# An LRU layer and a routed feed-forward on one core: the final stage adds both expert results to x1 in PSUM, and statistics and scaling read PSUM

## The reference

```python
x = _layernorm(x + LRU(x))      # x + x + sigmoid(res_logit) * gelu(y @ W1) @ W2, y from a complex linear recurrence
x = _layernorm(x + FFN(x))      # the stage of the change
# FFN: softmax over 8 experts, the two best per token, each with its weight
for e in range(8):
    h = gelu_exact(xf @ W1[e] + b1[e]);  y = h @ W2[e] + b2[e]
    out = out + y * cw[:, e:e + 1]
# _layernorm(x) = (x - mean) / sqrt(var + 1e-5) over the 128 features
```

## Time and profile before

| what | value |
|---|---|
| runs of the kernel before | 400.19, 402.85, 404.06 us; median 402.85 |
| the profiled execution, span from its first to its last instruction | 403.5 us |
| busy: PE, DVE, ACT, POOL | 75%, 73%, 64%, 65% of the span |
| indirect DMAs issued by POOL | 64 of L431, 108 of L437 |
| instructions | 6693 |

### The profile page before, as it was taken

The page is one execution under the profiler, slowest core; times in us unless marked ns, Lnnn a source line. Parts: engine busy times, 40 slices in busy tenths (PEclk is TensorE's granted clock), DMA queues, the critical chain, the costliest instruction groups (busy, mean ns, idle before and its releaser), DMA issues.

```text
span 403.5 us, 6693 instructions
## 1 busy us (share of the span) xinstructions
PE 301.3 (75%) x1531; PEld 253.2 (63%) x1531; DVE 295.8 (73%) x787; ACT 259.8 (64%) x569; POOL 263.2 (65%) x297
## 2 busy tenths in 40 slices
PE   2368999869874788899993599999999999100440
PEld 1235777546653677799993599999999995000110
DVE  3998999998653799899995289999999995100160
ACT  3315688378563687899994389999999993000451
POOL 4793479508877010577787777877877777777560
PEclk9999999899996699899999599999999999855585
DMA  4736516700111210223321332333333361111772
GB/s 116 268 95 220 173 39 220 281 1 33 48 47 37 56 42 20 67 74 88 87 69 54 85 92 79 85 85 83 84 89 89 92 199 52 52 52 52 190 215 78
DMA packets 47627, 39.23 MB, mean 97 GB/s; under 512 B 5160, under 2 KB 40240, under 8 KB 47608
## 3 DMA queue, kind: packets, MB, share of 16 engines
q1 hardware_dynamic: 42104, 27.68, 23.9%
q0 software_dynamic: 5504, 11.35, 8.6%
HBM read 18.39 MB, written 20.62 MB: 97 GB/s over the span
## 4 chain that ended last, share of the span: by engine, by line
POOL 32%; PE 29%; DVE 13%; issue 13%; ACT 6%; DMA 5%; SPq 0%; DVEq 0%; ACTq 0%; POOLq 0%
POOL slots_d L431 17%; POOL results_d L437 13%; PE bank L1016 8%; PE bank L1018 7%; PE bank L1017 7%; PE bank L1102 2%; DVE work L688 1%; PE bank L1119 1%; ACT fw L611 1%; DMA late<-slots_d 1%; DMA slots_d<-rows,slot_i 1%; ACT h L515 1%; DVE wuse L878 1%; DVE work L682 1%; DMA logs<-in_L_attn_res_logit_dram 1%
## 5 line engine op out<-in xcount | busy, mean ns | idle before, releaser
L437 POOL DMA_INDIRECT results_d<-work,dest x108 | 119.2, 1103 | 33.0 <-issue 32.0
L431 POOL DMA_INDIRECT slots_d<-rows,slot_i x64 | 72.1, 1127 | 49.4 <-DVE rows L834 19.1
L569 ACT ACTIVATE h<-bank,buse 128x384 f32<-128x384 f32 x144 | 84.1, 584 | 7.1 <-PE bank L1018 3.7
L915 DVE TENSOR_TENSOR h_l<-h,h_h 128x384 fp32r<-128x384 f32 x144 | 80.0, 556 | 6.3 <-ACT h_h L574 3.3
L1016 PE MATMUL bank<-h_h,wuse 128*128 128x384 f32 (+1 forms) x176 | 70.6, 401 | 3.9 <-DVE h_l L915 2.4
L1017 PE MATMUL bank<-h_l,wuse 128*128 128x384 f32 (+1 forms) x176 | 62.0, 352 | 0.0
L1018 PE MATMUL bank<-h_h,wuse 128*128 128x384 f32 (+1 forms) x176 | 61.9, 352 | 0.0
L1016 PE MATMUL bank<-xt_h,wuse 128*128 128x384 f32 x144 | 50.6, 351 | 3.7 <-ACT h L569 2.4
L878 DVE CAST wuse<-fw 128x1024 fp32r x72 | 49.8, 692 | 0.8 <-issue 0.8
L1017 PE MATMUL bank<-xt_l,wuse 128*128 128x384 f32 x144 | 49.5, 344 | 0.0
L1018 PE MATMUL bank<-xt_h,wuse 128*128 128x384 f32 x144 | 49.5, 344 | 0.0
(11 more groups left out here) (204 smaller groups left out, 651.8 us busy)
## 6 DMA issues: line engine op xcount, KB each, us to landing
late<-slots_d SPq DMA_DIRECT2D x36, 195.0 KB
late<-in_L_ffn_W_dram SPq DMA_DIRECT2D x16, 256.0 KB, 2.8
slots_d<-zeros SPq DMA_DIRECT2D x3, 1300.0 KB, 7.8
slots_d<-zeros SPq DMA_DIRECT2D x3, 1040.0 KB, 6.8
work<-results_d SPq DMA_DIRECT2D x10, 256.0 KB, 5.5
work<-in_L_attn_x3d_dram SPq DMA_DIRECT2D x8, 256.0 KB, 3.4
out_dram<-fw SPq DMA_DIRECT2D x8, 256.0 KB, 3.1
results_d<-work,dest POOLq DMA_INDIRECT x108
```

The lines of the kernel that those rows point to most:

```text
L431: pool.indirect_dma_start(out=slots_d, out_offset=bass.IndirectOffsetOnAxis(ap=slot_i[:, k, i:i + 1], axis=0), in_=rows[:, k, i, :], in_of ...
L437: pool.indirect_dma_start(out=results_d, out_offset=bass.IndirectOffsetOnAxis(ap=dest[:, SQ * g + q:SQ * g + q + 1], axis=0), in_=yo[:, g ...
L569: act.activation(h32[:, b % 2, 0:SLOTS], H_PS[b % 2][:, 0:SLOTS], ACT.Gelu, bias=buse[:, k, b:b + 1]).then_inc(sm["gelu_b"], 1)
L915: dve.tensor_tensor(ht_l[b], h32[:, b % 2, 0:SLOTS], ht_h[b].bitcast(F32), ALU.subtract).then_inc(sm["hbl_ready"], 1)
```

## The change

In the final stage PE now multiplies the identity by y1 as well, into the same bank behind y0, and raises `f_sum` after it. DVE's addition, `r3`, `f_r` and `f_res_last` go. Statistics and the scaling read the PSUM bank through `sum_of(c, q)`. ACT does all four tiles of the last chunk. `x1_sum` waits for `f_res` where it waited for `f_r`. In DVE's list `final_stats(c)` takes the place of `final_sum(c)`, and with it stands ahead of the aggregate of the chunk before.

```diff
-        r3 = late[:, 0:FB * CHUNK].rearrange("p (k q d) -> p k q d", k=FB, q=QT)
+        def sum_of(c, q):
+            return SUM_PS[c % len(SUM_PS)][:, q * D:(q + 1) * D]
...
             for c in range(NCH):
                 sp.wait_ge(sm["f_res"], c + 1)
-                if c == NCH - 1:
-                    sp.wait_ge(sm["f_res_last"], 1)
                 sp.dma_start(out_t[c], res[:, c]).then_inc(stored, 16)
...
             def final_apply(c, k):
                 act.wait_ge(sm["f_nmr"], c + 1)
-                for q in range(QT if c < NCH - 1 else QT // 2):
-                    last = act.activation(res[:, c, q, :], r3[:, k, q, :], ACT.Identity, bias=f_nmr[:, k, q:q + 1], scale=f_rstd[:, k, q:q + 1])
+                for q in range(QT):
+                    last = act.activation(res[:, c, q, :], sum_of(c, q), ACT.Identity, bias=f_nmr[:, k, q:q + 1], scale=f_rstd[:, k, q:q + 1])
                 last.then_inc(sm["f_res"], 1)
...
-            def final_sum(c, k):
-
-                wait(dve, sm["f_res"], c + 1 - FB)
+            def final_stats(c, k):
+
+                wait(dve, sm["f_nmr"], c + 1 - FB)
                 dve.wait_ge(sm["f_sum"], c + 1)
-                dve.wait_ge(y1_loaded[c], 16)
-                dve.tensor_tensor(r3[:, k].rearrange("p q d -> p (q d)"), SUM_PS[c % len(SUM_PS)][:], y01(c)[:, 1], ALU.add).then_inc(sm["f_r"], 1)
-
-            def final_stats(c, k):
-                dve.wait_ge(sm["f_r"], c + 1)
                 for q in range(QT):
-                    dve.bn_stats(f_st6[:, k, q, :], r3[:, k, q, :]).then_inc(sm["f_st"], 1)
+                    dve.bn_stats(f_st6[:, k, q, :], sum_of(c, q)).then_inc(sm["f_st"], 1)
...
             for c in range(NCH):
-                final_sum(c, c % FB)
+                final_stats(c, c % FB)
                 if c > late_from:
                     final_aggregate(c - 1, (c - 1) % FB)
-                final_stats(c, c % FB)
                 if c < late_from or c == NCH - 1:
                     final_aggregate(c, c % FB)
-
-            c, k = NCH - 1, (NCH - 1) % FB
-            dve.wait_ge(sm["f_nmr"], NCH)
-            for q in range(QT // 2, QT):
-                ins = dve.tensor_scalar(res[:, c, q, :], r3[:, k, q, :], f_rstd[:, k, q:q + 1], f_nmr[:, k, q:q + 1], ALU.mult, ALU.add)
-            ins.then_inc(sm["f_res_last"], 1)
...
             def x1_sum(c):
 
-                wait(pe, sm["f_r"], c + 1 - len(SUM_PS))
+                wait(pe, sm["f_res"], c + 1 - len(SUM_PS))
...
                 pe.wait_ge(y0_loaded[c], 16)
-                mm(SUM_PS[c % len(SUM_PS)][:], ident[:], y01(c)[:, 0], start=False, stop=True).then_inc(sm["f_sum"], 1)
+                mm(SUM_PS[c % len(SUM_PS)][:], ident[:], y01(c)[:, 0], start=False, stop=False)
+                pe.wait_ge(y1_loaded[c], 16)
+                mm(SUM_PS[c % len(SUM_PS)][:], ident[:], y01(c)[:, 1], start=False, stop=True).then_inc(sm["f_sum"], 1)
```

More of the change, by code:

```diff
@@ L231, in build @@
             zb_ready yt_ready yT_ready yo_ready
-            f_sum f_r f_st f_mv f_ve f_rstd f_nmr f_res f_res_last""".split()
+            f_sum f_st f_mv f_ve f_rstd f_nmr f_res""".split()
         sm = {n: sem(n) for n in names}
```

## The result

The changed kernel is slower. Over 20 runs of each it took 407.11 us against 404.63 (medians), 2.5 us more. The ratio on record is 1.0086, with a 95% interval of 1.0061 to 1.0110, so 3.5 us (2.5 to 4.5); it is not the quotient of the two medians, which is 1.0061. The forecast was 405.1 us on a base of 402.85, a ratio of 1.0056, with slower by over 1% at 0.19. Every one of the 20 runs of the changed kernel takes 2.1 to 2.2 us more than its span. For 31 runs of the kernel before on such a chip the spans are on record: 20 take 1.9 to 2.0 us more, four 3.1 to 3.6, and the median is 1.98. So 0.2 us of the difference are outside the span, where no profile shows them; the rest is in the span, and its end is what has to be explained.

The account below looks back on a forecast made before the run. POOL's closing DRAIN, fixed at 9.1 us behind its last norm, was taken to set the end. The norm's +2.3 us made 403.5 into 405.8 for the profiled execution, 405.1 on the median 402.85; own range 403.3 to 407.0, with rivals 401.8 to 408.0.

Parts of the forecast that it names:

- base of 402.85: Median time in us of three runs of the kernel before, to which the forecast added its 2.3 us.
- slower by over 1%: Outcome above 406.9 us, given 0.19: nearly all of B and a ninth of the forecast.
- The end is POOL's DRAIN behind its last norm: End of the span: POOL's closing DRAIN keeps its 9.1 us and moves with the last norm, by 2.3 us.
- Rival A: End of the span: POOL's DRAIN ends at its own time, so no change, 402.9 us; chance 0.17.
- The stage: Final stage, PE through DVE to POOL: chunk 4's norm starts 2.1 us later, the last norm ends 2.3 us later.
- y1(3) had landed: Chunk 3's second load on PE: taken as landed before its turn at 380.76, adding 1.71 us at half clock.
- the waits on ACT: PE's x1 of chunks 6 and 7 wait for ACT's bank reads, done 1.5 us ahead: nothing.
- B: PE at y1(3): a late load keeps the lower clock longer, 407.9 us, or 413 at half clock throughout; chance 0.12.
- C: PE in the final stage: clock up early, chunk 4's norm starts sooner, -0.8 us, 402.1 us; chance 0.06.
- The rule on PSUM reads: DVE's statistics: dearer PSUM access would put the end about 0.3 us later; the forecast assumed no difference.
- +2.3 us: End of POOL's last norm: 396.7 against 394.37, passed on whole to the end of the kernel.
- Worth nothing: Chunks 0 to 2: six more PE instructions, 2.6 us, hidden before PE's idle time; at most 2.6 us without that cover.

Follow-up runs that it names:

- a2_norms: Changed kernel with POOL's final norms moved to ACT and DVE and each aggregate behind its own statistics; 0.9882 of the kernel before.
- a3_warm: Changed kernel with 36 products into an idle bank ahead of y0(3), to keep PE busy until its loads land; 0.9988 of the kernel before.
- before_again: The kernel before, unchanged, profiled on a slower chip; 17.52 us from issue of the y0(3) load to the last norm's end.
- a1_order: Changed kernel with only DVE's order set back, aggregate ahead of the next chunk's statistics; 0.9983 of the kernel before.
- b1_order: Kernel before with only DVE's order changed, the aggregate behind the next chunk's statistics, sum still first; 0.9997 of the kernel before.
- after_third: The changed kernel, unchanged, profiled on the same chip as before_again; 18.57 us from issue of the y0(3) load to the last norm's end.
- after_again: The changed kernel, unchanged, timed again beside the kernel before on a slower chip; 1.0079 of the kernel before.

## Why the prediction was right and wrong

- *The end is POOL's DRAIN behind its last norm.* Right: 9.145 and 9.147 us, and a2_norms shows that it hangs on POOL's own last instruction alone. Rival A (it ends at its own time) is dead.
- *The stage.* Right step by step. Behind the first y0(3) product I had stats(5) at 9.95 us, aggregate(4) at 10.74, chunk 4's norm at 11.19 and the last norm's end at 17.8; they came at 9.83, 10.64, 11.08 and 17.64. The clock rose 5.25 us behind that product (5.55 before), y1(3) had landed, the waits on ACT cost nothing. Rivals B and C did not occur; a3_warm shows that C's mechanism is real. That B decides from 1 us of idling on, no run shows: in a3_warm PE idled 1.76 us and the clock stayed up, in before_again it idled 1.87 us and the clock fell 0.9 us behind y0(3).
- *What the cost is made of.* I had named both parts, PE's later sums and the aggregate behind the next chunk's statistics, but priced them together. a1_order and b1_order part them: 1.1 to 1.3 us are the order, 0.8 to 1.0 PE's added work.
- *The rule on PSUM reads.* `bn_stats` took 280 ns from PSUM (276 from SBUF before), so the measurement decides against the 0.3 us that I had worked out by the Trainium skill's Perfetto Trace Analysis, Optimizing Scalar/DVE Operations. An activation took 457 ns (478 before).
- *The step that failed is the sum, from the profile to the runs.* It has two terms, a base and +2.3 us, and both came out low. The base of 402.85 is the median of three runs; over 20 it is 404.63. I had held a span, 403.5, against these times, as if the two were one quantity; with the 1.9 to 2.2 us that runs take beyond their spans, the profiled execution took some 405.5 us by my estimate, more than any of the three, so it doesn't lie among them as the part on the time before has it. Had the +2.3 been put on 404.63, it would be 406.9 against 407.11 measured. The change itself was told as 0.56%, within what this kernel's runs can tell from nothing (about 1%). The runs showed 0.86% (0.61 to 1.10), clear of zero and of 0.56%: 20 runs of each tell 0.25%. So the term of 2.3 us was too small: by the ratio it is 3.5 us (2.5 to 4.5), of which the final stage measured 2.2 and 0.2 are outside the span. I had priced nothing outside the final stage. Whether the rest, up to 1.1 us, is real stays open; by the medians it is 0.1 us.
- *A cover that was taken for granted.* "Worth nothing" for the six instructions of chunks 0 to 2 rested on PE's idle 33.9 us. On the other two chips that idle time does not exist: PE works on x1 until 404.15 in after_third and starts y0(3) 3.63 us behind the issue instead of 3.09. By that the added instructions cost 0.5 us of the 1.05 there; it was not tried apart.

## What to carry to other kernels

Look first at what each queue does last, its closing DRAIN included: here 8.9 us stood behind POOL's last instruction, outputs had 5 us of slack, and moving eight chunks' small norms to other engines was worth more than anything done to the sums. When an operation is taken out of an engine's list, read its neighbours again: the aggregate had stood behind a sum that was ready and came to stand behind statistics that had to wait for PE, and that was 1.1 to 1.3 of the 2.2 us. Relieving an engine pays only if what it feeds does not come later. And before two profiles are compared to a few tenths of a microsecond, look at when the clock rose in each.

## What the runs showed of the hardware that was not expected

POOL's closing DRAIN is over 8.84 to 8.96 us behind POOL's last work in all sixteen runs and both first profiles (its start is given to 0.1 us), whether the last work is a tensor instruction or an indirect DMA, and whatever else runs.

The same kernel takes 405 us on one chip and 425 to 431 on others. The difference is in the middle stage. The stretch from 200 to 250 us, first in the kernel before on the first chip, then in after_again:

```profile
200.00:250.00 50.00, 38.76 (x226) 37.45 (x226) 34.90 (x89) 35.09 (x82) 39.05 (x36) 0.90 0.28 80
```
```profile
200.00:250.00 50.00, 10.49 (x30) 8.06 (x30) 4.94 (x12) 5.59 (x12) 32.72 (x34) 0.50 0.16 50
```

PE is busy for 10.5 us of the 50 instead of 38.8, and DVE and ACT for 5 instead of 35, while POOL goes on. At the end of the longest of these waits ACT goes on first and PE behind it:

```profile
217.29 0.58 ACT L556 ACTIVATE rt<-bank,buse 128x384 f32<-128x384 f32 x1 [16.21 <-remote]
218.00 0.90 PE L1107 MATMUL bank<-ident,rt 128*128 128x128 f32 x3 [15.54 <-ACT rt L556]
```

The word remote stands for a semaphore event behind which the profile has neither an instruction nor a transfer. ACT has such waits, of up to 24 us, in all twelve profiles of the two slower chips and in none of the six of the first. Their cause was not looked for. By the profiles they bear on what a change of the final stage is worth, since behind them PE has no long idle time left before its loads are issued.
